# A sixteen-expert MoE in whole float32: two 64-row products on the two row halves of TensorE, in place of a split into rounded parts

## What is computed

```python
def _L1_ffn_ref(x, gate_w, gate_b, w1, w2, w3):
    logits = jnp.einsum('bsd,de->bse', x, gate_w) + gate_b
    probs = jax.nn.softmax(logits, axis=-1)
    top_probs, top_idx = jax.lax.top_k(probs, 2)
    top_probs = top_probs / jnp.sum(top_probs, axis=-1, keepdims=True)
    dispatch = jnp.sum(jax.nn.one_hot(top_idx, n_experts, dtype=x.dtype) * top_probs[..., None], axis=-2)
    h1 = jnp.einsum('bsd,edh->bseh', x, w1)
    h2 = jnp.einsum('bsd,edh->bseh', x, w2)
    hidden = jax.nn.silu(h1) * h2
    expert_out = jnp.einsum('bseh,eho->bseo', hidden, w3)
    return jnp.einsum('bseo,bse->bso', expert_out, dispatch)

    t = t + _L1_ffn_ref(_ln_t(t), L1_ffn_gate_w, L1_ffn_gate_b, L1_ffn_w1, L1_ffn_w2, L1_ffn_w3)
```

## Time and profile before

| | |
|---|---|
| three runs | 834.64 us median (832.77 to 834.84) |
| the profiled execution | 837.63 us, of which 835.9 us are the traced span |
| PE, DVE, ACT, POOL busy | 80%, 62%, 47%, 31% of the span |
| instructions | 11024 |

### The profile page before, as it was taken

The page is one execution under the profiler, slowest core; times in us unless marked ns, Lnnn a source line. Parts: engine busy times, 40 slices in busy tenths (PEclk is TensorE's granted clock), DMA queues, the critical chain, the costliest instruction groups (busy, mean ns, idle before and its releaser), DMA issues.

```text
span 835.9 us, 11024 instructions
## 1 busy us (share of the span) xinstructions
PE 670.5 (80%) x2972; PEld 439.8 (53%) x2972; DVE 514.1 (62%) x1481; ACT 395.9 (47%) x846; POOL 255.2 (31%) x331
## 2 busy tenths in 40 slices
PE   5795958858799999999957997558999997763772
PEld 4554744357655555555536776555445543642531
DVE  6536599657887777777745565764433435375447
ACT  3331256644564444444425454354666665434445
POOL 7400154425045344444330000530333243141004
PEclk9885557955599999999969989755999999885685
DMA  5600000002063344244210000021222120000001
GB/s 127 106 1 0 1 0 0 1 1 51 2 156 77 82 101 98 58 97 100 51 32 2 1 1 1 0 43 42 70 71 76 51 76 25 2 0 1 1 0 50
DMA packets 24430, 34.61 MB, mean 41 GB/s; under 512 B 10888, under 2 KB 20128, under 8 KB 22272
## 3 DMA queue, kind: packets, MB, share of 16 engines
q1 hardware_dynamic: 24384, 34.05, 17.4%
HBM read 32.60 MB, written 1.44 MB: 41 GB/s over the span
## 4 chain that ended last, share of the span: by engine, by line
PE 59%; DVE 21%; ACT 7%; issue 5%; POOL 4%; DVEq 1%; DMA 1%; ACTq 0%; SPq 0%; POOLq 0%
PE ps L1620 12%; PE ps L2193 8%; PE ps L2209 7%; PE ps L1641 5%; PE ps L593 4%; PE ps L740 2%; DVE ST L491 2%; PE ps L2309 2%; DVE tok_split L588 2%; PE ps L1098 2%; POOL rstd L513 1%; PE ps L765 1%; PE ps L1909 1%; PE ps L2566 1%; PE ps L1921 1%
## 5 line engine op out<-in xcount | busy, mean ns | idle before, releaser
L1354 POOL TENSOR_TENSOR out_acc<-out_acc,tok_tmp 128x512 f32<-128x512 f32 x80 | 103.5, 1294 | 237.5 <-DVE tok_tmp L1546 126.6
L1620 PE MATMUL ps<-tokT,w 128*128 128x512 f32 x512 | 136.9, 414 | 2.4 <-ACT act_buf L1592 1.4
L1620 PEld LDWEIGHTS ps<-tokT,w 128*128 128x128 f32 x512 | 94.5, 194 | 51.8 <-issue 24.3
L1592 ACT ACTIVATE act_buf<-ps 128x512 f32<-128x512 f32 x128 | 76.0, 597 | 91.5 <-PE ps L1620 88.5
L511 POOL TENSOR_TENSOR nmean<-mean2x,neghalf 128x8 f32<-128x8 f32 x32 | 8.1, 254 | 283.8 <-DVE var L498 283.7
L593 PE MATMUL ps<-ident,tok_split 128*128 128x128 f32 x224 | 48.6, 389 | 52.6 <-DVE tok_split L588 42.7
L2193 PE MATMUL ps<-tokT,w 128*128 128x512 f32 x256 | 70.8, 421 | 2.8 <-ACT hid_buf L2171 2.8
L593 PEld LDWEIGHTS ps<-ident,tok_split 128*128 128x128 f32 x224 | 39.4, 204 | 57.5 <-DVE tok_split L588 40.7
L2193 PEld LDWEIGHTS ps<-tokT,w 128*128 128x128 f32 x256 | 47.9, 197 | 31.0 <-ACT hid_buf L2171 14.8
L513 POOL TENSOR_TENSOR rstd<-vpe,neghalf 128x8 f32<-128x8 f32 x32 | 55.1, 1722 | 2.7
L1541 DVE TENSOR_TENSOR hid_buf<-act_buf,ps 128x512 f32<-128x512 f32 x64 | 43.5, 686 | 20.2 <-ACT act_buf L1592 16.0
(11 more groups left out here) (467 smaller groups left out, 1277.8 us busy)
## 6 DMA issues: line engine op xcount, KB each, us to landing
disp_all<-disp_dram SPq DMA_DIRECT2D x32, 512.0 KB, 6.2
disp_all<-disp_dram SPq DMA_DIRECT2D x32, 256.0 KB, 3.9
w_raw<-in_L_ffn_w SPq DMA_DIRECT2D x4, 512.0 KB, 8.7
XIN<-in_x SPq DMA_DIRECT2D x4, 256.0 KB, 3.6
w_raw<-in_L_ffn_W SPq DMA_DIRECT2D x2, 512.0 KB, 6.1
out<-XIN SPq DMA_DIRECT2D x4, 256.0 KB, 2.2
fc_raw<-in_L_conv_upfc_w SPq DMA_DIRECT2D x1, 512.0 KB, 4.8
w<-in_L_ffn_w SPq DMA_DIRECT2D x1, 512.0 KB, 10.5
```

The costliest lines, as they stand in the source:

```text
L1354: pool.tensor_tensor(out_acc[:, :], out_acc[:, :], weighed[p % 2], ALU.add).then_inc(mm["acc"].sem, 1)
L1592: act.activation(act_buf[e % 2][:, :], ps[:, e % 2, :], ACT.Silu).then_inc(mm["act"].sem, 1)
L1620: last = pe.matmul(ps[:, 2 * k + e % 2, :], w12[:, part, k, EXPERT1[e], :], tokT[:, bass.ts(i, CHUNK)], start=(part == 0), stop=(part == 1))
```

## The change

The tokens stay whole. ACT writes each normalised token twice, side by side, into `tok_split` (`norm_twice`), so that the transposed tile holds the same tokens on rows 0 to 63 and 64 to 127 of `tokF`, which is `tokT`'s memory as float32. There is no `split` and no wait of PE for one: PE's transposes wait for the normalisation itself (`xu`). `w1` is loaded onto rows 0 to 63 of `w12` and `w2` onto rows 64 to 127, once each, and used as loaded. In `hidden` the two whole-float32 products of an expert use rows 0 to 63 and rows 64 to 127 of the array, in different banks; both waits now stand ahead of both. The router uses whole tokens and gate weights on rows 0 to 63 (`router_whole`), so that `router_logits` has no two parts to add.

```diff
+        def norm_twice(act, g, rstd_sem, u_sem, ps_sem):
+            act.wait_ge(*rstd_sem(g + 1))
+            if g >= 2:
+                act.wait_ge(*ps_sem(2 * (g - 1)))
+            both = tok_split[g % 2][:, :, :, :].bitcast(F32)
+            for t in range(TG):
+                tt = g * TG + t
+                last = act.activation(both[:, t, :, :], X[:, tt, :].unsqueeze(1).to_broadcast([P, 2, C]), ACT.Identity,
+                                      bias=nmr[:, tt:tt + 1], scale=rstd[:, tt:tt + 1])
+            last.then_inc(u_sem.sem, 1)
...
+        def whole_scalar(act, rstd_sem, u_sem, ps_sem, ft_sem, then):
+            norm_twice(act, 0, rstd_sem, u_sem, ps_sem)
+            then(act)
+            for g in range(G):
+                if g + 1 < G:
+                    norm_twice(act, g + 1, rstd_sem, u_sem, ps_sem)
+                for j in (2 * g, 2 * g + 1):
+                    act.wait_ge(*ps_sem(j + 1))
+                    act.activation(tokF[:, j * CHUNK:(j + 1) * CHUNK], ps[:, j % 2, :], ACT.Copy).then_inc(ft_sem.sem, 1)
...
-                    e1_weights_scalar(act, j)
...
-            e1_weights_vector(dve)
...
+        def router_whole(pe, g, w, ne, bank, done):
+            for t in range(g * TG, (g + 1) * TG):
+                at = t * 2 * ne
+                last = pe.matmul(ps[:, bank + at // 512, at % 512:at % 512 + ne], tokF[0:C, t * P:(t + 1) * P], w[0:C, :],
+                                 start=True, stop=True)
+            last.then_inc(done.sem, 1)
...
-            vlink(dve.tensor_copy(rt[3], lp[:, :, 0, :]))
-            vlink(dve.tensor_tensor(rt[1], rt[3], lp[:, :, 1, :], ALU.add))
+            if not whole:
+                vlink(dve.tensor_copy(rt[3], lp[:, :, 0, :]))
+                vlink(dve.tensor_tensor(rt[1], rt[3], lp[:, :, 1, :], ALU.add))
...
-            for h in range(2):
-                for k, nm in enumerate(("L1_ffn_w1", "L1_ffn_w2")):
-                    wdma(sp, "w12", w12_raw[h * C:(h + 1) * C, k, :, :], a[nm].rearrange("e d h -> d e h"))
+            for k, nm in enumerate(("L1_ffn_w1", "L1_ffn_w2")):
+                wdma(sp, "w12", w12[k * C:(k + 1) * C, :, :], a[nm].rearrange("e d h -> d e h"))
...
-            ln_vector(dve, mm["rstd"], mm["xu"], mm["fs"], mm["ft_ps"], extra=lambda g, sl: prep_vector(dve, g), by_dve=0)
+            for g in range(G):
+                dve.wait_ge(*mm["xu"](g + 1))
+                prep_vector(dve, g)
...
-            ln_tensor(pe, mm["fs"], mm["ft_ps"], mm["ft"], then=lambda g: router_tensor(pe, g, gw2, E1, 6, mm["lg_ps"]))
+            ln_tensor(pe, mm["xu"], mm["ft_ps"], mm["ft"], then=lambda g: router_whole(pe, g, gw, E1, 6, mm["lg_ps"]))
             def hidden(i, e):
 
+                pe.wait_ge(*mm["act"](i * E1 + (e + 1)))
+                pe.wait_ge(*mm["m1"](i * E1 + (e + 1)))
                 for k in range(2):
-                    pe.wait_ge(*mm[("act", "m1")[k]](i * E1 + (e + 1)))
-                    for part in range(2):
-                        last = pe.matmul(ps[:, 2 * k + e % 2, :], w12[:, part, k, EXPERT1[e], :], tokT[:, bass.ts(i, CHUNK)],
-                                         start=(part == 0), stop=(part == 1))
-                    last.then_inc(mm[("h_ps", "h2_ps")[k]].sem, 1)
+                    rows = slice(k * C, (k + 1) * C)
+                    pe.matmul(ps[:, 2 * k + e % 2, :], w12[rows, EXPERT1[e], :], tokF[rows, i * CHUNK:(i + 1) * CHUNK],
+                              start=True, stop=True).then_inc(mm[("h_ps", "h2_ps")[k]].sem, 1)
...
-            e1_weights_pool(pool)
```

More of the change, by code:

```diff
@@ L128, in build @@
         tokT = sb("tokT", [P, TOK], F32R)
+        tokF = over("tokF", "tokT", [P, TOK])
         ST = sb("ST", [P, NT, 6])
@@ L1262, in router_transpose, with router_logits @@
             last.then_inc(mm["dt_ps"].sem, 1)
-        def router_logits(dve, mm, rts, half, ne, bias, bank, rescale=None):
+        def router_logits(dve, mm, rts, half, ne, bias, bank, rescale=None, whole=False):
             rt, tiles = rts[half], NT // len(rts)
@@ L1269, in router_logits @@
             lp = ps[:, bank, :].rearrange("p (t h e) -> p t h e", h=2, e=ne)
-            vlink(dve.tensor_copy(rt[3], lp[:, :, 0, :]))
-            vlink(dve.tensor_tensor(rt[1], rt[3], lp[:, :, 1, :], ALU.add))
+            if not whole:
+                vlink(dve.tensor_copy(rt[3], lp[:, :, 0, :]))
+                vlink(dve.tensor_tensor(rt[1], rt[3], lp[:, :, 1, :], ALU.add))
             if rescale is not None:
                 rescale(dve, rt[1], rt[2])
-            vlink(dve.tensor_tensor(rt[0], rt[1], bcm(bias, tiles), ALU.add))
+            vlink(dve.tensor_tensor(rt[0], lp[:, :, 0, :] if whole else rt[1], bcm(bias, tiles), ALU.add))
             vlink(dve.tensor_reduce(r[0], rt[0], X_AXIS, ALU.max))
@@ L1381, in build @@
         prep = signals((1, "filled ln bias_ps bias att"), (E2, "hi lo"))
-        s_w12 = sem("w12_split")
-        s_w12h = sem("w12_hi")
-        s_gw = sem("gw_split")
         def e1_sync(sp):
-            for h in range(2):
-                wdma(sp, "gw", gw[h * C:(h + 1) * C, :], a["L1_ffn_gate_w"])
+            wdma(sp, "gw", gw[0:C, :], a["L1_ffn_gate_w"])
             wdma(sp, "gw", b_gw[:, :], a["L1_ffn_gate_b"].unsqueeze(0).to_broadcast([P, E1]))
-            for h in range(2):
-                for k, nm in enumerate(("L1_ffn_w1", "L1_ffn_w2")):
-                    wdma(sp, "w12", w12_raw[h * C:(h + 1) * C, k, :, :], a[nm].rearrange("e d h -> d e h"))
+            for k, nm in enumerate(("L1_ffn_w1", "L1_ffn_w2")):
+                wdma(sp, "w12", w12[k * C:(k + 1) * C, :, :], a[nm].rearrange("e d h -> d e h"))
             wdma(sp, "w3", w3[:, :, :], a["L1_ffn_w3"].rearrange("e h o -> h e o"))
[L1396 to L1403, removed]
-            k, i = step // 4, step % 4
-            if step == 0:
-                wwait(act, "w12")
-            act.activation(w12[:, 0, k, 4 * i:4 * i + 4, :], w12_raw[:, k, 4 * i:4 * i + 4, :], ACT.Copy).then_inc(s_w12h, 1)
-        def e1_weights_pool(pool):
-            for k in range(2):
-                for i in range(4):
-                    sl = slice(4 * i, 4 * i + 4)
-                    pool.wait_ge(s_w12h, 4 * k + i + 1)
-                    pool.tensor_tensor(w12[:, 1, k, sl, :], w12_raw[:, k, sl, :], w12[:, 0, k, sl, :].bitcast(F32),
-                                       ALU.subtract).then_inc(s_w12, 1)
         def e1_pool(pool):
@@ L1524, in e1_vector @@
             mm = e1
[L1525 removed]
+            for g in range(G):
+                dve.wait_ge(*mm["xu"](g + 1))
+                prep_vector(dve, g)
+            wwait(dve, "gw")
             dve.sem_inc(mm["m1"].sem, 2)
@@ L1528, in e1_vector @@
             dve.sem_inc(mm["ta"].sem, 1)
-            router_logits(dve, mm, route1, 0, E1, b_gw[:, :], 6)
+            router_logits(dve, mm, route1, 0, E1, b_gw[:, :], 6, whole=True)
             for step in range(5):
                 router_top2(dve, mm, route1, 0, E1, step)
-            router_logits(dve, mm, route1, 1, E1, b_gw[:, :], 7)
+            router_logits(dve, mm, route1, 1, E1, b_gw[:, :], 7, whole=True)
             for step in range(5, TOP2_STEPS):
@@ L1582, in e1_scalar @@
             mm = e1
-            ln_scalar(act, mm["rstd"], mm["xu"], mm["ft_ps"], mm["ft"], by_dve=0, then=prep_ln)
+            whole_scalar(act, mm["rstd"], mm["xu"], mm["ft_ps"], mm["ft"], then=prep_ln)
             act.sem_inc(mm["act"].sem, 2)
```

10 lines of the change are left out of this document (4 added, 6 removed).

## The result

The changed kernel takes 855.49 us (median of 4 runs, 854.61 to 856.76) against 833.70 for the kernel before (4 runs, 832.47 to 834.84): ratio 1.0263, 95% interval 1.0239 to 1.0287, slower by 20 to 24 us. Forecast were 855 us and a range of 845 to 880.

The account below looks back on a forecast made before the run. PE was taken to set the experts' pace, through a chain of waits. Losses of 16.6 us there and 2.9 us ahead of it sum to 19.5 us, giving 855 us against the median of 834.64; range 845 to 880.

Parts of the forecast that it names:

- The two terms: Losses forecast in the experts, +16.6 us, and ahead of the experts, +2.9 us; together 19.5 us.
- what was not counted: Experts: DVE's addition of a chunk between two gates delays a stalled product about 0.1 us a chunk, about +1 us.
- A whole record holds its half for 0.43 us, an expert takes 0.86, from the column halves: Experts on PE: row halves overlap as `outp`'s column halves do; 0.86 us an expert, gaining 0.29 us per four experts.
- The stall of 0.80, the quad +0.52: Four experts plus `outp` (a quad): PE waits 0.80 us for expert 0's gate before expert 2; 6.31 us from 5.79.
- 32 equal quads: Experts: all 32 groups of four experts, four in each of 8 chunks, lose 0.52 us each, +16.6 us.
- Router +2.9 us: Ahead of the experts: whole router products, 3.47 us per eight tiles, delay the dispatch transposes from 226.02 to 228.9, +2.9 us.
- Weights, loads and ACT's wider normalisation at nothing: Earlier blocks and token preparation: dropped weight roundings, halved loads and wider normalisation writes are covered by other work, zero.
- Everything behind the experts unchanged: Attention and later blocks: the forecast sum had no term for them.
- Rival A, records in order of issue: Experts: w2 product starts only with w1's second record; one stall more, +13.8 us, 869; chance 0.11 with partial overlap.
- Rival B, one behind the other: Experts: row halves do not overlap, an expert takes 1.72 us, about 938 us; chance 0.13.
- The loss of four row tiles carried over to two: Experts: the skill's 3.07 for four row tiles, applied to two, makes a pair a third longer, above 890; no separate chance.
- Rival C, records of 64 rows under 0.33 us: Experts: whole records on half the rows as brief as rounded ones, 0.22 to 0.23 us; 815 us; chance 0.05.

Follow-up runs that it names:

- Waits apart: Changed kernel with the wait for the gate ahead of the w2 product only, each product waiting for its own bank, two banks: 852.90 us, ratio 1.0232.
- one wait: Changed kernel without PE's wait for the silu of expert e-2 ahead of the products, which the gate's wait implies: 858.09 us, ratio 1.0290.
- the changed kernel with all its repairs: Changed kernel with a third w2 bank from the first chunk, router products on both row halves, and the normalisation moved: 829.78 us, ratio 0.9949.

## Why the prediction was right

The mechanism was as forecast, in its place: row halves at the same time, a stall ahead of the third expert of a quad, ended by a gate on DVE. A third bank took the chunk's loss away (27.27 to 24.56) and did little for the kernel before (24.69 to 24.26). That the number came within 1 us is in part luck. The two terms were too small by 5 us together (24.5 for 19.5, with 1 more taken for what was not counted). Against that stood a gift of the clock in attention, 7 us in the profiled pair and about 3 between the medians, which no step of the prediction had.

- *A whole record holds its half for 0.43 us, an expert takes 0.86, from the column halves:* right (330.00 and 330.43). Without a stall, sixteen records take 3.73 us in place of 3.93, a gain of 0.20 a quad; I had 0.29.
- *The stall of 0.80, the quad +0.52:* the mechanism right, the size too small. In the quad of 6.58, the third expert starts 2.72 us behind the first (331.83 - 329.11), for which I had 2.52, and the second pair takes 1.99 for which I had 1.92, so 6.58 in place of 6.31. The step that was off is the sentence that `weigh` isn't short of time. It is not, by the share of its time (DVE 69% busy), but in this quad it stands ahead of the gate in DVE's queue, itself held up by the statistics, and the gate comes 0.22 behind the silu in place of 0.035. That is nearly all of the 0.20. In the quad with `back` the gate comes 0.12 behind, with DVE idle before it, and in the quad of 6.64 it comes 0.03 behind. There DVE's addition of the chunk stands between two gates (352.05 to 352.63), and expert 3 of the quad starts 1.09 us behind expert 2, where it starts 0.93 behind in the quad of 6.58. That is 0.16 a chunk, 1.3 us in all, the term that I had put at about +1. All this is read from the timeline. No kernel had the `weigh`, the statistics or the addition elsewhere.
- *32 equal quads:* wrong both ways. The quad at the chunk's boundary did not grow (6.76 for 6.79), because silu(0) was already held up there by the normalisation, and the stall lies under that delay in part. With the norm moved the kernel before shows the delay by its absence (5.81), and so does the changed kernel with its third bank (6.00). With two banks the changed kernel was not run so. The quad with `back` grew by 0.96, 0.8 like its neighbours and some 0.16 more. A chunk: 0.79 - 0.03 + 0.96 + 0.84 = 2.56, where I had 2.08; over 8 chunks 20.5 us in place of 16.6.
- *Router +2.9 us:* 4.0. A group of products was right (3.53 between starts, I had 3.47). The step that was off is the eight transposes at 1.61 us. Ahead of whole products they take 1.87 (207.14 - 205.27), 0.26 more, three times. ACT's normalisation takes the 0.40 a tile that I took (3.17 us for eight tiles), and PE has no gap. From the logits to the dispatch transposes pass 4.62 us (229.72 - 225.10), as taken.
- *Weights, loads and ACT's wider normalisation at nothing:* the second transposes start at 205.27 and 202.67 us in the two profiles of the changed kernel, and at 205.57 and 203.72 in those of the kernel before. A gain of more than a microsecond or so is not in this, and a smaller one can't be told from chance.
- *Everything behind the experts unchanged:* in work, yes; in time, no, 7 us by the clock. No step named this.
- *Rival A, records in order of issue:* false. The w2 product's first record starts with the w1 product's first, ahead of its second. Expert 0's two pairs start at 329.04 and 329.57, and the second ends at 330.17. Were a pair the two records of one product, the w1 product would be done with the first pair, and its silu would not wait until 330.19. The Trainium skill ("TensorE: Matmul & The Clock Gate", Part 3, The mechanism) has matmuls start and end in program order; by this trace it holds for instructions and not for the two records that each whole product has.
- *Rival B, one behind the other:* false for the changed kernel, and its price was right when brought about (941.57 us for 938).
- *The loss of four row tiles carried over to two (above 890):* the runs are against it. Sixteen records take 3.73 us on two halves and 7.06 on one, 1.89 times. The Trainium skill ("TensorE: Matmul & The Clock Gate", Measured speedup vs the span model) has 3.07 for four tiles, and no run here had four.
- *Rival C, records of 64 rows under 0.33 us:* false, 0.43.

What stays open is the clock in attention. It was 0.92 in both profiled executions of the changed kernel, 0.86 and 0.87 in those of the kernel before, and 0.86 to 0.89 in those of the ten other kernels. Waits apart and one wait should have saved 6 and 2 us by their chunks, and the medians say -2.6 and +2.6. The mean clock of the whole execution is on record for each run. It was 0.827 to 0.831 in all five of the changed kernel, and 0.815 to 0.829 in the six of one wait, whose shortest (854.77 us) is the one at 0.829. So the gift seems to be in every measured run of the changed kernel, and in few of one wait. Why is not known, and it isn't a property of the edit that one could plan with.

## What to carry to other kernels

When two products that ran one behind the other become simultaneous, count the turn of each buffer anew: first record to silu to gate to the next product, against the work that PE has in between. If it is longer, a third bank is what is missing, before any gain of the array can show. In that count look at what stands ahead of the consumer in its own queue, even on an engine with time to spare. And compare stages, not only times. Here up to 7 us came back from a block that nobody had touched, and of a repair of 6 us it let 2.6 be seen.

## What the runs showed that I had not expected

The same 464 PE instructions of the attention block took 96 to 104 us from kernel to kernel, at mean granted clocks of 0.92 to 0.86, with nothing changed in them. That is up to 8 us, more than most edits here. Row halves overlap for whole float32 records completely, 0.43 us a pair of records, and for the router's 16 columns at half clock as well (1.90 us in place of 3.59). And an edit to a part that neither kernel had touched, the place of the normalisation on ACT, made the kernel before 0.44% faster, as fast as the changed kernel with all its repairs.
